# Attention by halves of a head, with six entries of lead, values three entries behind

## What is computed

```python
q, k, v = (proj(x).reshape(b, l, 16, 8).transpose(0, 2, 1, 3) for proj in (Wq, Wk, Wv))
q, k = rope(q), rope(k)
scores = jnp.einsum('bhsd,bhed->bhse', q, k) / np.sqrt(8)
attn = jax.nn.softmax(scores, axis=-1)
out = jnp.einsum('bhse,bhed->bhsd', attn, v)
return out.transpose(0, 2, 1, 3).reshape(b, l, 128) @ Wo.T + bo
```

## Time and profile before

| | us |
|---|---|
| median of 3 runs | 1122.44 (1120.43 to 1123.07) |
| the profiled execution | 1119.95 |
| its span | 1117.3 |
| first exponential of attention starts | 395.3 |
| last exponential of attention starts | 974.6 |

### The profile page before, as it was taken

How to read it: one execution, slowest core, us unless ns; L and a number is a source line. 1 busy time by engine, 2 the same in 40 slices (tenths; PEclk the granted TensorE clock), 3 DMA queues, 4 the chain that set the end, 5 groups by cost and what they waited for, 6 DMA issues and landing times.

```text
span 1117.3 us, 22178 instructions
## 1 busy us (share of the span) xinstructions
PE 1010.8 (90%) x8304; PEld 473.2 (42%) x8304; DVE 839.2 (75%) x1538; ACT 783.3 (70%) x1108; POOL 289.8 (26%) x296
## 2 busy tenths in 40 slices
PE   9937767998998799999999999999999999989994
PEld 6512223698954222332223222322332222247994
DVE  2599997526746789999999999999999996073113
ACT  3663433265545679999999999999999999931222
POOL 0068892575626300000000000000000000006772
PEclk8969999899989889999999999999999999989997
DMA  3056541764142221001110111011101100028633
GB/s 110 1 161 205 189 150 38 250 179 139 45 170 98 91 63 36 9 29 36 36 22 17 36 36 31 7 37 36 36 2 35 36 4 2 4 69 267 197 99 134
DMA packets 57973, 87.91 MB, mean 79 GB/s; under 512 B 26240, under 2 KB 28664, under 8 KB 57484
## 3 DMA queue, kind: packets, MB, share of 16 engines
q1 hardware_dynamic: 50542, 73.42, 21.5%
q0 software_dynamic: 4544, 9.32, 2.8%
q10 hardware_dynamic: 2782, 3.77, 1.0%
HBM read 73.10 MB, written 12.94 MB: 77 GB/s over the span
## 4 chain that ended last, share of the span: by engine, by line
PE 68%; DVE 10%; issue 8%; DMA 4%; ACT 4%; POOL 3%; SPq 1%; ACTq 0%; POOLq 0%; DVEq 0%
PE psum L990 24%; PE psum L976 22%; PE psum L1104 6%; PE psum L1124 5%; PE psum L980 2%; PE psum L785 2%; DVE ssm_h L1781 2%; DVE tile_max L2065 2%; PE psum L820 1%; PE psum L1084 1%; DMA w1r<-y_dram 1%; POOL y_dram L1590 1%; ACT hid L1426 1%; DMA q_stack<-max_parts 1%; PE psum L800 1%
## 5 line engine op out<-in xcount | busy, mean ns | idle before, releaser
L1364 ACT ACTIVATE probs<-psum 128x1024 f32<-128x1024 f32 x512 | 505.5, 1040 | 15.2 <-PE psum L980 4.3
L2065 DVE TENSOR_REDUCE tile_max<-psum 128x1 f32<-128x512 f32 x720 | 456.5, 684 | 27.9 <-PE psum L976 26.4
L990 PE MATMUL psum<-probs,v_head 128*32 128x256 f32 (+1 forms) x3840 | 321.0, 406 | 0.7 <-ACT probs L1364 0.4
L976 PE MATMUL psum<-k_stack,q_stack 62*128 62x512 bf16 x994 | 311.0, 397 | 11.1 <-DMA q_stack<-q_dram 7.8
L980 PE MATMUL psum<-q_stack,k_stack 64*128 64x512 bf16 x1024 | 302.9, 384 | 4.3 <-DMA q_stack<-max_parts 3.9
L976 PEld LDWEIGHTS psum<-k_stack,q_stack 62*128 62x128 bf16 x994 | 92.0, 110 | 246.0 <-DVE tile_max L2065 116.6
L1562 POOL TENSOR_TENSOR max_parts<-row_max,no_shift 128x8 bf16<-128x8 f32 x32 | 6.4, 201 | 537.9 <-DVE row_max L2041 537.9
L990 PEld LDWEIGHTS psum<-probs,v_head 128*32 128x32 f32 x3840 | 75.7, 108 | 154.8 <-issue 110.3
L1104 PE MATMUL psum<-x_cols,w1r 128*128 128x128 f32 (+1 forms) x624 | 78.2, 278 | 9.8 <-ACT hid L1426 4.6
L1510 POOL TENSOR_TENSOR h0T<-dtuT,ssm_b 128x1024 f32<-128x1024 f32 x32 | 76.9, 2417 | 16.4 <-DVE ssm_h L1781 7.3
L1104 PEld LDWEIGHTS psum<-x_cols,w1r 128*128 128x128 f32 x624 | 72.9, 192 | 12.4 <-ACT hid L1426 5.6
(11 more groups left out here) (289 smaller groups left out, 1068.0 us busy)
## 6 DMA issues: line engine op xcount, KB each, us to landing
w1r<-w SPq DMA_DIRECT2D x78, 256.0 KB, 3.5
ssm_b<-bc_dram SPq DMA_DIRECT2D x32, 512.0 KB, 4.0
k_stack<-k_dram SPq DMA_DIRECT2D x60, 120.0 KB
w_held<-w SPq DMA_DIRECT2D x16, 256.0 KB, 5.1
q_stack<-q_dram SPq DMA_DIRECT2D x30, 96.0 KB
bc_p<-bc_dram SPq DMA_DIRECT2D x5, 512.0 KB, 5.7
xtok_dram<-x_tok SPq DMA_DIRECT2D x8, 256.0 KB, 2.4
w1r<-y_dram SPq DMA_DIRECT2D x8, 256.0 KB, 5.3
```

The lines of the kernel that those rows point to most:

```text
L976: mm(bank, queries, k_stack[rows, u, keys:keys + C], start=True, stop=True).then_inc(s1_ps, 1)
L990: i = mm(psum[32 * j:32 * j + VM, 7, lo:hi], v_head[:, u, kt, :], probs[:, kt % 4, j * C + lo:j * C + hi], start=kt == 0, stop=kt == KT - ...
L1364: f(probs[:, kt % 4, hf * HALF:(hf + 1) * HALF], banks(2 * slot, 2), ACT.Exp, scale=SCALE).then_inc(p_ready, 1)
L2065: v.tensor_reduce(top, bank, AX.X, ALU.max).then_inc(s1_read, 1)
```

## The change

`entry(kt, hf)` becomes `KT * hf + kt`: a head is two units of 16 entries, first all key tiles of the first query half and then all of the second. `probs` is eight slots of 1024 columns. Values go by units, always 256 columns a group, three entries behind the exponentials; each unit has its own `keep` of 256 columns and its own five stores (`STORES`, the stores of one head, goes from 5 to 10). The maxima run ahead by half a head and `LEAD` = 6 entries: 32 + 12 = 44 tiles precede the first entry. The first head keeps its own order and six banks for 32 tiles and takes the common order and the ring of three after them. The rows of head 0's first half are issued by ACT, behind the copies of the first 32 tiles; SP waits for them before it loads the stacks of head 1. Afterwards SP issues, for each unit, the stores of the unit before and the rows of the next unit. The core of the diff:

```diff
-STORES = NC + 1
+QUARTER = C // 2
+STORES = 2 * (NC + 1)
+PROBS = 8
-FIRST_MAXIMA = first_order()
+UNIT = SN // 2
+FIRST_MAXIMA = first_order()[:UNIT] + MAXIMA[UNIT:]
-LEAD = 4
+LEAD = 6
 def bank_of(hs, p):
-    return 4 + (hs + p) % RING if hs else FIRST_BANKS[p % len(FIRST_BANKS)]
+    return 4 + (hs + p) % RING if hs or p >= UNIT else FIRST_BANKS[p % len(FIRST_BANKS)]
 def entry(kt, hf):
-    return 2 * kt + hf
+    return KT * hf + kt
-        probs = attn_sb("probs", [128, 4, L])
+        probs = attn_sb("probs", [128, PROBS, HALF])
...
                 sp.wait_ge(stacks_clear, 3)
+                sp.wait_ge(rows_in[0], ROW_LOADS)
                 load_q(sp, 1, 1)
                 load_k(sp, 1, 1)
-                load_rows(sp, 0, 0, 0)
-                load_q(sp, 2, 2)
-                load_k(sp, 2, 2)
-                for u in range(3, UN):
-                    load_q(sp, u, u)
-                    load_k(sp, u, u)
...
                 for h in range(NH):
-                    if h:
-                        store_head(h - 1)
-                    if h + 1 < NH:
-                        for hf in range(2):
-                            load_rows(sp, h + 1, (h + 1) % UN, hf)
+                    for hf in range(2):
+                        if h or hf:
+                            store(h - 1 + hf, 1 - hf)
+                        following = h + hf
+                        if following < NH:
+                            load_rows(sp, following, following % UN, 1 - hf)
+                        if h == 0:
+                            load_q(sp, hf + 2, hf + 2)
+                            load_k(sp, hf + 2, hf + 2)
...
+                def values(h, hf, kt):
+                    n = h * ENTRIES + entry(kt, hf)
                     if kt == 0:
+                        if hf == 0:
+                            pe.wait_ge(v_head_ready, h + 1)
+                        pe.wait_ge(o_copied, 2 * h + hf + 1)
+                    pe.wait_ge(p_ready, n + 3)
                     for j in range(NC):
+                        i = mm(psum[32 * j:32 * j + VM, 7, unit_cols(hf)], v_head[:, h % UN, kt, :],
+                               probs[:, n % PROBS, j * QUARTER:(j + 1) * QUARTER], start=kt == 0, stop=kt == KT - 1, skip_group_check=True)
+                    i.then_inc(pv_done, 1)
+
+                def late_values(h, hf, kt):
+
+                    if kt < 2:
+                        if h or hf:
+                            values(h - 1 + hf, 1 - hf, KT - 3 + kt)
+                            if kt:
+                                values(h - 1 + hf, 1 - hf, KT - 1)
+                    elif kt == 3:
+                        values(h, hf, 0)
+                        values(h, hf, 1)
+                    elif kt > 4:
+                        values(h, hf, kt - 3)
...
-                for p in range(SN):
+                for p in range(UNIT + 2 * LEAD):
                     if p == FIRST_BANKS.index(1):
                         pe.wait_ge(v_all_ready, TILES)
                     maxima(0, 0, p)
-                for p in range(2 * LEAD):
-                    maxima(1, 1, p)
...
-                for p in range(SN):
+                for p in range(UNIT + 2 * LEAD):
+                    if p == UNIT:
+                        load_rows(act, 0, 0, 0)
                     if FIRST_MAXIMA[p][3] == APART:
                         above(0, p)
-                above(1, 0)
-                load_rows(act, 0, 0, 1)
                 for h in range(NH):
...
+                    for hf in range(2):
+                        for kt in range(KT):
+                            ahead = UNIT + 2 * (h * ENTRIES + entry(kt, hf) + LEAD)
+                            if ahead % GROUP == 0 and ahead < NH * SN:
+                                above(ahead // SN, ahead % SN)
+                            exponentials(h, hf, kt)
+                            if kt == 1 and (h or hf):
+                                keep(h - 1 + hf, 1 - hf)
...
-                        if p == SN // 2 + 1:
-                            row_maxima(hs, 0)
-                    row_maxima(hs, 1)
+                        if p % UNIT == UNIT - 1:
+                            row_maxima(hs, p // UNIT)
```

More of the change, by code:

```diff
@@ L989, in values @@
                     for j in range(NC):
[L990 to L1005, removed]
@@ new lines, in late_values, with unit, ahead @@
+                def late_values(h, hf, kt):
[9 more added lines that the diff above has]
+                        values(h, hf, kt - 3)
+                def unit(h, hf):
+                    u = h % UN
+                    def ahead(kt):
+                        at = UNIT + 2 * (h * ENTRIES + entry(kt, hf) + LEAD)
+                        if at >= NH * SN:
@@ L1012, in ahead @@
                             return [lambda: None] * 2
-                        return [lambda p=p: maxima(h + d, (u + d) % UN, p, turn + (u + d) // UN) for p in (2 * q, 2 * q + 1)]
+                        hs = at // SN
+                        return [lambda p=p: maxima(hs, hs % UN, p, hs // UN) for p in (at % SN, at % SN + 1)]
                     for kt in range(KT):
[L1016 to L1027, removed]
@@ L1028, in attention @@
-                for p in range(SN):
+                        upper, lower = ahead(kt)
+                        upper()
+                        n = entry(kt, hf)
+                        if kt == 0:
+                            pe.wait_ge(rows_in[hf], h * ROW_LOADS + ROW_LOADS)
+                        pe.wait_ge(p_ready, h * ENTRIES + (n + 1))
+                        scores(u, kt, hf, n % 2, 1)
+                        scores(u, kt, hf, n % 2, 0).then_inc(s2_ps, 1)
+                        lower()
@@ L1029, in attention @@
+                        late_values(h, hf, kt)
+                for p in range(UNIT + 2 * LEAD):
                     if p == FIRST_BANKS.index(1):
@@ L1031, in attention @@
                     maxima(0, 0, p)
-                for p in range(2 * LEAD):
-                    maxima(1, 1, p)
                 for h in range(NH):
-                    head(h, h % UN, h // UN, following=NH - 1 - h)
-                values(NH - 1, UN - 1, KT - 2, 1)
-                values(NH - 1, UN - 1, KT - 1)
+                    for hf in range(2):
+                        unit(h, hf)
+                for kt in range(KT - 3, KT):
+                    values(NH - 1, 1, kt)
             def attention_out():
@@ L1374, in attention @@
                         above(0, p)
-                above(1, 0)
-                load_rows(act, 0, 0, 1)
                 for h in range(NH):
-                    for kt in range(KT):
-                        ahead = h * SN + SN + 4 * kt + 2 * LEAD
-                        if ahead % GROUP == 0 and ahead < NH * SN:
-                            above(ahead // SN, ahead % SN)
-                        for hf in range(2):
-                            exponentials(h, kt, hf)
-                        if kt == 0 and h:
-                            keep(h - 1)
@@ L1386, in attention @@
-                keep(NH - 1)
-                act.wait_ge(o_copied, 1 + NH)
-                store_chunks(act, NH - 1, LAST_BY_ACT)
+                    for hf in range(2):
+                        for kt in range(KT):
[5 more added lines that the diff above has]
+                                keep(h - 1 + hf, 1 - hf)
```

88 lines of the change are left out of this document (43 added, 45 removed).

## The result

The changed kernel takes 1128.47 us (median of 6 runs, 1126.86 to 1134.5), beside 1120.86 for the kernel before in the same series: ratio 1.0082, with 0.6% to 1.0% more as its 95% interval (1.0061 to 1.0103). The forecast was 1129.0, 6.5 more than before; measured are 7.6 more. That 1128.47 lies only 0.5 from 1129.0 is in part luck: the forecast stood on 1122.44 for the kernel before, which is 1.6 more than this series gave. The span of the profiled execution is 1125.9, before 1117.3.

A forecast was written before the change was run, and what follows sets the result against it. PE's instruction order was taken to bound attention. Boundaries +9.4, rows -1.8, end without maxima +2.8, prologue -3.3 and tail -0.6 sum to +6.5, put on the median 1122.44: 1129.0 us, range 1118 to 1137.

The forecast's parts named there:

- PE's order sets the pace: Steady attention: PE's instruction order gives 1.12 us an entry; DVE has 0.18 to spare in four entries, ACT 0.25.
- (a): Unit boundaries in attention: 0.53 us lost at each of 30, 15.9 against 6.5 now, net +9.4.
- the walk: Entry-by-entry timing of a unit's boundary by rules read from the trace: entry 8 at 9.52 us, where steady is 8.98.
- (b): Row loads in attention: with a lead of six, rows arrive in 7.0 of 7.86 us, ending waits: -1.8.
- SP done near entry 8: SP's queue: a unit's stores and a head's stack loads, 9.7 us, end near entry 8, before entry 9's row maximum.
- the 2.0 to land: Last part of the rows' way after their four issues: landing takes 2.0 us of the 7.0.
- (c): End of attention: entries without maxima, 0.92 us instead of 1.12, fall from 36 to 22: +2.8.
- (d): Prologue: 44 maxima tiles instead of 72, but ACT blocked behind POOL's product and PE at half clock: -3.3.
- (e): After the last exponential: half a V and half a keep remain, -0.6 us.
- B: Rival: boundaries half as dear because keep is halved; 1119.8 us, chance 0.12.
- C: Rival: drains at tiling-mode switches decide, so time goes by PE's own work; 1112 us, chance 0.11.
- D: Rival: prologue gives nothing back, through blocked ACT and half clock to entry 8 or later, or late stacks; 1135, chance 0.11.

The follow-up runs named there:

- E11: Changed kernel with values (V) always in pairs, two tiles in every odd entry and none in even ones: 1167.02 us, one run.
- E1: Changed kernel with V of a unit's tile 1 moved from entry 3 to entry 4: 1117.73 us, ratio to the kernel before 0.9963.
- E2: Changed kernel with keep done twice in each unit, an extra 256-column copy to a scratch tile ahead of the real one: 1137.64 us, one run.
- E3: Changed kernel with LEAD 8 and not 6: 1127.34 us, one run.
- E4: Changed kernel with LEAD 4 and not 6: 1159.40 us, one run.
- E8: Kernel before, with the full V of entry 3 of each head split over entries 3 and 4: ratio to the kernel before 0.9973.
- E5: Changed kernel with the first row loads of head 0 issued by SP and not by ACT: 1124.27 us, one run.
- E6: E5 plus POOL's product over xT put behind the first row maxima of head 0 on POOL's queue: 1121.45 us, one run.
- E10: Changed kernel with head 3's stacks loaded before the rows of head 1's first half and not after them: 1127.66 us, one run.
- the last kernel: Changed kernel with the edits of E1, E5, E6 and E10 together: 1107.88 us, ratio to the kernel before 0.9886.

## Why the prediction was right, point by point

*PE's order sets the pace.* Right. A steady entry stays at 1.12. E11 shows the same engine with less work and more time.

*(a) Boundaries.* Right in mechanism and size. 18.51 a unit against 18.50; each wait of the walk is in the rows, and the times above agree with it within 0.02. E1, E2, E3 and E11 move it by 0.36, 0.25, 0.08 and 1.31, against expected 0.35, 0.3, 0.08 and 1.7. The price of two half V in a row, 1.00, was taken from the end of attention, and not from twice the single one; with 1.14 the sum would have been 9 too high.

*(b) Rows.* Half right. In the steady units no wait for rows is left, as worked out, and E4 shows what the lead is for. The spare time was put at 0.8. The last landing was counted 0.6 too long for it (E4), and in every other unit, from 5 to 23, the four issues take 3.1 to 3.6 and not 2.47: there the rows land only 0.2 to 0.7 ahead of the score, and 1.4 ahead in most others. And the prediction looked at a steady head only. In head 0 two units pay 0.47 and 0.70 more than the rest, together 1.2, which covers the miss of the middle part (+11.37 against +10.4). For the 0.70 the step that failed is the one that has SP done near entry 8, before the row maximum: two heads' stacks stand in its queue there. For the 0.47 it is the 2.0 to land, which was 3.73 for one load. How much of the -1.8 is in a usual execution of the kernel before is not known either (E8).

*(c) The end without maxima.* It stands in the same part of the table, and nothing there contradicts it: the last 21 steps from one exponential to the next take 19.43, 0.93 each, where 0.92 was expected. It was not tested by itself.

*(d) Prologue.* -2.97 against -3.3. The chain was as told: product on POOL until 386.3, rows on ACT's queue, copies behind them, DVE idle for 7.30, half clock, exponential 0 13.7 after the row maximum (14.3 in the walk). E5 and E6 show both causes, 4.1 and 3.0.

*(e) The tail.* -1.08 against -0.6. The ten other kernels with the changed tail spread over 141.7 to 143.0 there, and the kernel before has 142.7, so neither number can be told from nothing.

*The rivals.* B is refuted by E2 and the unit's 18.51, C by E1 and E11. C leaned on the Trainium skill's page "TensorEngine Tiling (Array Packing)", section "Tiling Modes", by which a change of the tiling mode drains the engine. The rows fit that rule (two sets of V in a row cost 1.00, two with scores between them 2 × 0.57), but the drains were not what the time hung on. D did not occur: the clock was back at 400.7.

## What to carry to other kernels

In an engine that keeps its order, an even spacing of what its neighbours feed on can be worth more than less work: moving one V out of a double entry gained 0.36 us a unit at the cost of a switch, and pairing all of them lost 1.3. Walk one period, with each buffer's release written down, and check the walk on the trace of before; what it gives for the new order can be trusted to a few hundredths, while for an order not walked a guess was off by more than a factor of three. A transfer issued from a busy engine's queue blocks what stands behind it for as long as it waits: give it to the queue that is idle, and look at the first periods apart from the steady one. Moving a block of transfers ahead on a queue that is full moves the wait to what then stands behind it (E10, and the last kernel). When durations are added up along a chain, see from where each was counted: a landing counted from its issue holds the issue already.

## What the runs showed of the hardware

Two half-width sets of four column groups in fp32 cost 1.00 us in a row and 0.57 each alone, so a pair in a row is 0.14 cheaper than two with scores between them.

PE's granted clock fell to half in the prologue even where PE was never idle long. In the kernel with POOL's product moved (E6) it was 0.50 for 10.2 us, from 382.9 on; just before that and until 386.3 PE issued one maxima tile of 512 columns about every 0.6 us.

A row load of 1 KB took about 0.6 us of the issuing queue and landed 2.0 us (median) after the start of its issue, 1.9 at the least and 3.7 at the most (changed kernel).
